# Window attention in the last two layers: copies on the DMA queue, squares after the rotation, masks before the wait for q and k, weights first on GpSimd

## The reference, cut to what is computed here

```
h = shift_token(x)                      # upper 64 features come from the token before
q, k, v = split(h @ wqkv)               # 8 heads of 64 numbers each
q, k = l2norm(q) * q_scale, l2norm(k) * k_scale
q, k = rotary_xpos(q, k)                # q * cos + rotate_half(q) * sin, with scales
# windows of 64 tokens; a query sees its own window and the one before
sim  = 8 * q . k, masked outside i - 64 <= j <= i
o    = softmax(sim) @ v
x    = x + o @ wo
h    = layernorm(shift_token(x)) @ w1 + b1
a, g = split(h)
x    = x + (a * gelu(g)) @ w2 + b2
```

## Time and profile before

| | us |
|---|---|
| median of 3 runs | 1512.03 |
| lowest and highest | 1510.12, 1512.65 |
| the profiled execution, its own time | 1508.53 |
| its span (first to last instruction) | 1506.5 |
| PE busy | 1333.5 (89%) |
| DVE busy | 1013.3 (67%) |
| ACT busy | 792.7 (53%) |
| POOL busy | 361.6 (24%) |

### The profile page before, as it was taken

How to read it: one execution, slowest core, us unless ns; L and a number is a source line. 1 busy time by engine, 2 the same in 40 slices (tenths; PEclk the granted TensorE clock), 3 DMA queues, 4 the chain that set the end, 5 groups by cost and what they waited for, 6 DMA issues and landing times.

```text
span 1506.5 us, 23829 instructions
## 1 busy us (share of the span) xinstructions
PE 1333.5 (89%) x9009; PEld 790.8 (52%) x9009; DVE 1013.3 (67%) x2202; ACT 792.7 (53%) x1681; POOL 361.6 (24%) x288
## 2 busy tenths in 40 slices
PE   6999999999999999999589999987279988799886
PEld 4767677776777673333223333333146654366652
DVE  5767767687766856765577667740967775877755
ACT  4544435444444442434136666675169984499851
POOL 0000000011000003335410000000267771477732
PEclk9999999999999999999569999999589999999998
DMA  5000000000000000002023111100200000000000
GB/s 141 1 1 1 1 1 1 1 1 1 1 1 1 0 1 1 1 0 81 29 77 82 46 37 37 36 3 7 57 1 2 2 2 1 1 2 2 2 1 28
DMA packets 23725, 26.03 MB, mean 17 GB/s; under 512 B 5602, under 2 KB 20140, under 8 KB 22316
## 3 DMA queue, kind: packets, MB, share of 16 engines
q1 hardware_dynamic: 23612, 24.51, 5.5%
HBM read 20.11 MB, written 4.39 MB: 16 GB/s over the span
## 4 chain that ended last, share of the span: by engine, by line
PE 64%; ACT 14%; DVE 13%; issue 4%; POOL 2%; DMA 2%; SPq 0%; POOLq 0%; DVEq 0%; ACTq 0%
PE ps L679 13%; PE ps L699 8%; PE ps L714 7%; ACT probsT L2283 6%; PE ps L1051 4%; PE ps L1010 4%; PE ps L1031 3%; DVE negmax L1437 2%; PE ps L888 2%; PE ps L882 2%; PE ps L1182 2%; PE ps L650 2%; ACT v_st L2253 2%; PE ps L1173 2%; PE ps L872 2%
## 5 line engine op out<-in xcount | busy, mean ns | idle before, releaser
L2208 ACT ACTIVATE probsT<-ps 128x512 f32<-128x512 f32 (+1 forms) x304 | 163.6, 576 | 103.7 <-PE ps L1035 91.6
L1437 DVE TENSOR_REDUCE negmax<-ps 128x1 f32<-128x1024 f32 x128 | 150.7, 1219 | 72.5 <-PE ps L699 72.4
L2030 ACT ACTIVATE probs<-ps,negmax 128x1024 f32<-128x1024 f32 x128 | 142.5, 1114 | 80.5 <-DVE negmax L1437 76.5
L2036 ACT COPY probsT<-ps 128x512 f32<-128x512 f32 x128 | 74.8, 584 | 168.2 <-PE ps L714 168.1
L714 PEld LDWEIGHTS ps<-ident,probs 128*128 128x128 f32 x1024 | 114.5, 141 | 66.2 <-issue 44.0
L714 PE MATMUL ps<-ident,probs 128*128 128x128 f32 x1024 | 138.4, 277 | 6.6 <-DVE probsT L1450 3.4
L2360 POOL TENSOR_SCALAR rstd<-mv 128x4 f32<-128x4 f32 (+1 forms) x23 | 5.3, 233 | 578.5 <-DVE mv L1372 578.4
L1010 PE MATMUL ps<-arena 76*128 76x512 bf16 (+3 forms) x384 | 113.6, 355 | 26.4 <-DVE cmax L1705 20.6
L699 PE MATMUL ps<-k_st,q_st 64*128 64x512 f32 x512 | 128.7, 622 | 5.9 <-ACT probs L2030 5.9
L1705 DVE CUSTOM_DVE_ANT_0 k_st<-ps,rel 128x256 f32<-128x256 f32 (+7 forms) x128 | 96.8, 756 | 44.1 <-PE ps L1010 43.2
L1705 DVE CUSTOM_DVE_ANT_0 q_st<-ps,rel 128x256 f32<-128x256 f32 (+7 forms) x128 | 96.7, 756 | 41.9 <-PE ps L1010 41.0
(11 more groups left out here) (245 smaller groups left out, 2565.1 us busy)
## 6 DMA issues: line engine op xcount, KB each, us to landing
arena<-c_parts SPq DMA_DIRECT2D x32, 192.0 KB
arena<-c_parts SPq DMA_DIRECT2D x16, 128.0 KB
arena<-in_L_ffn_w_dram SPq DMA_DIRECT2D x3, 512.0 KB
c_parts<-probsT SPq DMA_DIRECT2D x2, 768.0 KB, 3.5
arena<-in_c_far_dram SPq DMA_DIRECT2D x16, 96.0 KB
c_parts<-work SPq DMA_DIRECT2D x2, 768.0 KB, 11.3
work<-in_L_ffn_wqkv_dram SPq DMA_DIRECT2D x1, 1536.0 KB
x_sb<-in_L_attn_x_dram SPq DMA_DIRECT2D x2, 512.0 KB, 5.9
```

What stands on the lines that cost most here:

```text
L1437: dve.tensor_reduce(negmax[:, u:u + 1], s2, AX_X, ALU.max, negate=True).then_inc(s_a_negmax, 1)
L2030: act.activation(probs[:, u % NPB, :], s2, ACT.Exp, bias=negmax[:, u:u + 1], accum_out=rowsum[:, u:u + 1]).then_inc(s_a_exp, 1)
L2208: act.activation(c_p[:, kt % 2, j0:j0 + heads, q0 - kt * P:q0 - kt * P + n], ps[:, 4 + c % 2, 0:heads * n].rearrange("p (h n) -> p h n", n ...
```

## The change

- `d_vs` is no longer written by ACT. SP issues two DMAs for each tile: rows 0 to 63 from `d_va` of the tile, and rows 64 to 127 from `d_va` of the tile before. A new semaphore `s_d_vs` counts them; `shifted(n)` is its value when all copies of the tiles before tile n have landed. ACT waits for `shifted(n)` before it writes `d_va` of tile n, since the copies of tile n - 1 read the buffer that is written. PE waits for it ahead of the weights times v. `s_d_v` now comes with the one remaining copy.
- `square` moves on ACT from behind the exponentials to behind the value copy, for tile t + 2 instead of t + 3, and waits for the rotation (`s_d_m`) instead of the projection. `rotate` on DVE waits for the projection (`s_d_qkp`) instead of the squares. `norms` waits for the squares, and stands behind the addition to x.
- On PE the waits for turned q and k move from ahead of the two mask matmuls to behind them. The wait for `s_d_e` stays ahead.
- On POOL `unit_norm` loses its first addition, which becomes `add_queries`. A step is now: weights of tile t, power and scaling of tile t + 2, and then the addition of q for tile t + 3. `add_keys` and `add_queries` wait for `s_d_qkt`, the turn of the tile that used the buffer before.

```diff
--- before.py
+++ after.py
@@ -422,6 +422,7 @@
         s_d_kT = sem("s_d_kT")
         s_d_v = sem("s_d_v")
         s_d_addk = sem("s_d_addk")
+        s_d_vs = sem("s_d_vs")
         s_d_s = sem("s_d_s")
         s_d_nm = sem("s_d_nm")
         s_d_nm8 = sem("s_d_nm8")
@@ -453,6 +454,13 @@
         STACK = 16 * 9
 
         block = ctx.enter_context(nc.Block())
+
+        def exists(t, shift):
+            return 0 <= t + shift < TILES
+
+        def shifted(n):
+
+            return 16 * (2 * n - (n + TILES - 1) // TILES)
 
         @block.sync
         def _(sp):
@@ -550,6 +558,18 @@
                 for m, w in enumerate(("L1_ffn_q_scale", "L1_ffn_k_scale")):
                     sp.dma_start(qk_scale[:, l, m, :], a[w][l].partition_broadcast(P)).then_inc(s_ld_d, 16)
 
+            for l in range(DEPTH):
+                for t in range(TILES):
+                    n, par = TILES * l + t, t % 2
+                    sp.wait_ge(s_d_v, n + 1)
+                    if exists(t, -2):
+                        sp.wait_ge(s_d_o, n - 1)
+                    if n:
+                        sp.wait_ge(s_d_vs, shifted(n))
+                    sp.dma_start(d_vs[0:WIN, par, :], d_va[0:WIN, par, :]).then_inc(s_d_vs, 16)
+                    if exists(t, -1):
+                        sp.dma_start(d_vs[WIN:P, par, :], d_va[WIN:P, 1 - par, :]).then_inc(s_d_vs, 16)
+
             for b in range(BATCH):
                 for g in range(HALF):
                     sp.wait_ge(s_res, group_no(3, b, g))
@@ -560,8 +580,6 @@
 
         NU = 2 * QT
 
-        def exists(t, shift):
-            return 0 <= t + shift < TILES
 
         def ring(j):
 
@@ -1151,8 +1169,6 @@
                             pe.wait_ge(s_d_v, n)
                         pe.matmul(ps[:, 3, :], hT[:, WIN + t * P:WIN + (t + 1) * P], w4qkv[:, l, 2 * INNER:3 * INNER],
                                   start=True, stop=True).then_inc(s_d_vp, 1)
-                        pe.wait_ge(s_d_qT, n + 1)
-                        pe.wait_ge(s_d_kT, n + 1)
                     if exists(t, 0):
 
 
@@ -1162,6 +1178,8 @@
                             pe.matmul(ps[:, 6 + i, :].rearrange("p (h c) -> p h c", c=P), ident_b[:, :],
                                       mask_b[:, t:t + 1, :].to_broadcast([P, 4, P]),
                                       start=True, stop=False, skip_group_check=True)
+                        pe.wait_ge(s_d_qT, n + 1)
+                        pe.wait_ge(s_d_kT, n + 1)
                         for h in range(H2):
                             r, m = HD2 * (h % 2), h // 2
 
@@ -1199,6 +1217,7 @@
 
                         pe.wait_ge(s_d_pTa, n)
                         pe.wait_ge(s_d_pT, n)
+                        pe.wait_ge(s_d_vs, shifted(n))
                         pe.wait_ge(s_d_v, n)
                         if exists(t, -2):
                             pe.wait_ge(s_d_oT, n - 1)
@@ -1774,7 +1793,7 @@
 
                         return v.rearrange("p t n d -> p n t d").to_broadcast([P, 2, H2, v.shape[3]])
 
-                    dve.wait_ge(s_d_sq, n + 1)
+                    dve.wait_ge(s_d_qkp, n + 1)
                     if exists(t, -2):
                         dve.wait_ge(s_d_add, n - 1)
                     dve.tensor_tensor(mA, qk, heads(rot_c[:, t:t + 1, :, :]), ALU.mult)
@@ -1785,12 +1804,15 @@
 
             def add_keys(l, t):
                     n, par = TILES * l + t, t % 2
+                    if exists(t, -2):
+                        dve.wait_ge(s_d_qkt, n - 1)
                     dve.wait_ge(s_d_m, n + 1)
                     dve.tensor_tensor(d_kq[par][:, INNER:2 * INNER], d_mA[:, par, INNER:2 * INNER],
                                       d_mB[:, par, INNER:2 * INNER], ALU.add).then_inc(s_d_addk, 1)
 
             def norms(l, t):
                     n, par = TILES * l + t, t % 2
+                    dve.wait_ge(s_d_sq, n + 1)
                     dve.tensor_reduce(ss[:, par, :], d_sq[:, par, :].rearrange("p (h d) -> p h d", d=HD2),
                                       AX_X, ALU.add).then_inc(s_d_ss, 1)
                     dve.wait_ge(s_d_ss, n + 1)
@@ -1799,6 +1821,7 @@
 
             def step(l, t, piece=None):
                     n, par = TILES * l + t, t % 2
+
                     if exists(t, 2):
                         rotate(l, t + 2)
                     if exists(t, 0):
@@ -1816,12 +1839,13 @@
                            .then_inc(s_d_pT, 1)
                     if exists(t, 2):
                         add_keys(l, t + 2)
-                        norms(l, t + 2)
                     if exists(t, -2):
 
                         dve.wait_ge(s_d_w, n - 1)
                         z = xT[:, (t - 2) * P:(t - 1) * P]
                         dve.tensor_tensor(z, ps[:, 3, 0:P], z, ALU.add).then_inc(s_d_z, 1)
+                    if exists(t, 2):
+                        norms(l, t + 2)
                     if piece:
                         piece()
                     if exists(t, 0):
@@ -1936,9 +1960,9 @@
                     last_norm(0)
                 else:
                     add_keys(l + 1, 0)
-                    norms(l + 1, 0)
                 gated(l, 10)
                 if not last:
+                    norms(l + 1, 0)
                     next_shift(l, 1)
                 gated(l, 11)
                 add_down(l, 2)
@@ -2249,7 +2273,7 @@
                     n, par = TILES * l + t, t % 2
                     if exists(t, -2):
                         act.wait_ge(s_d_ss, n - 1)
-                    act.wait_ge(s_d_qkp, n + 1)
+                    act.wait_ge(s_d_m, n + 1)
                     act.activation(d_sq[:, par, :], ps[:, 0:2, :].rearrange("p n c -> p (n c)"), ACT.Square)\
                        .then_inc(s_d_sq, 1)
 
@@ -2267,12 +2291,14 @@
                     if piece:
                         piece()
                     if exists(t, 0):
-                        if exists(t, -1):
-                            act.wait_ge(s_d_v, n)
-                            act.copy(d_vs[WIN:P, par, :], d_va[WIN:P, 1 - par, :])
                         act.wait_ge(s_d_vp, n + 1)
-                        act.copy(d_va[:, par, :], ps[:, 3, :])
-                        act.copy(d_vs[0:WIN, par, :], ps[0:WIN, 3, :]).then_inc(s_d_v, 1)
+                        if n >= 2:
+                            act.wait_ge(s_d_vs, shifted(n))
+                        if exists(t, -2):
+                            act.wait_ge(s_d_o, n - 1)
+                        act.copy(d_va[:, par, :], ps[:, 3, :]).then_inc(s_d_v, 1)
+                    if exists(t, 2):
+                        square(l, t + 2)
                     if exists(t, -1):
                         act.wait_ge(s_d_pt, n)
                         act.copy(d_pT[:, 0:4, :].rearrange("p h c -> p (h c)"), ps[:, 4, :]).then_inc(s_d_pTa, 1)
@@ -2285,8 +2311,6 @@
                                                  scale=d_rn[:, par, hd:hd + 1],
                                                  accum_out=d_sum[:, par, h:h + 1])
                         ins.then_inc(s_d_e, 1)
-                    if exists(t, 3):
-                        square(l, t + 3)
 
 
             def ffn_yT(l, c):
@@ -2307,7 +2331,7 @@
 
             for l in range(DEPTH):
                 if l == 0:
-                    for t in range(3):
+                    for t in range(2):
                         square(l, t)
                 for t in range(15):
                     step(l, t)
@@ -2328,12 +2352,11 @@
                     if j == 6:
                         ffn_yT(l, 3)
                     if l + 1 < DEPTH:
-                        if j == 8:
+                        if j == 9:
                             square(l + 1, 0)
                 if l + 1 < DEPTH:
                     square(l + 1, 1)
                     act.activation(tpre[:, 1:2], eps_c[:, 0:1], ACT.Exp)
-                    square(l + 1, 2)
 
 
         @block.gpsimd
@@ -2477,33 +2500,47 @@
 
             pool.wait_ge(s_d_init, 1)
 
-            def unit_norm(l, t):
+            def add_queries(l, t):
 
                     n, par = TILES * l + t, t % 2
                     kq = d_kq[par]
                     pool.wait_ge(s_d_m, n + 1)
+                    if exists(t, -2):
+                        pool.wait_ge(s_d_qkt, n - 1)
                     pool.tensor_tensor(kq[:, 0:INNER], d_mA[:, par, 0:INNER], d_mB[:, par, 0:INNER], ALU.add)\
                         .then_inc(s_d_add, 1)
+
+            def unit_norm(l, t):
+
+                    n, par = TILES * l + t, t % 2
                     pool.wait_ge(s_d_cl, n + 1)
                     pool.tensor_tensor(d_rn[:, par, :], ss[:, par, :], half_c[:, :], ALU.pow).then_inc(s_d_rn, 1)
                     pool.wait_ge(s_d_addk, n + 1)
+                    pool.wait_ge(s_d_add, n + 1)
                     pool.wait_ge(s_d_rn, n + 1)
-                    v = kq[:, INNER:2 * INNER].rearrange("p (h d) -> p h d", d=HD2)
```

(27 more changed lines are left out.)

## The result

The changed kernel takes 1488.61 us (median of 4 runs, 1487.84 to 1488.89) where before takes 1512.12 (4 runs). The ratio is 0.9846, 95% interval 0.9829 to 0.9863: 23.5 us faster. 22.5 were forecast, 1489.5 us, in a range of 1484 to 1500.

The account below looks back on a forecast made before the run. A ring of waits through PE and ACT bounds the 9.04 us step, then PE's 8.41. 15.1 + 3.4 + 1.6 + 2.3 + 2.0 - 1.9 = 22.5 us off the median 1512.03 gives 1489.5, range 1484 to 1500.

Parts of the forecast that it names:

- twelve steps a layer, tile 1 to 13: Steady steps of both layers: each falls from 9.04 to 8.41 us, 15.1 in all; the second interval gives 0.3 more a layer.
- first interval, tile 0 to 1: Between the first two tiles, where PE has no output or weighted values to compute: 1.4 us less a layer.
- late steps, tile 13 to 15: Two steps a layer without projection of q and k: masks go under PE's wait for k, 4 x 0.4 = 1.6 us.
- from tile 15's maxima on, both layers: Tile 15 without half copies on ACT saves 2.3 us; between layers, rotations no longer behind the squares save 2.0.
- layer starts, meetings: Cost at layer starts: sums wait for later squares, 0.4 to 0.5 us each, and DVE and POOL meet; taken as 1.9.
- the ring: PE and ACT wait for each other: exponentials, squares, q/k copies, masks, scores, weights' turn and copy; 9.04 us falls to 7.6.
- The step, 8.41: Steady step after the change: PE is full and sets it at its own busy time, 8.41 us instead of 9.04.
- The bounds of the terms: Uncertainties: PE's step may be 8.3, 2.6 us less in all; TensorE's clock is worth some 2.5 us either way.
- Squares: On ACT, moved behind the value copy: 0.91 us leave the ring, at no cost while 0.6 us to spare lasts.
- Masks: On PE, ahead of the wait for k: 0.53 us leave the ring; that wait goes, with 0.1 us to spare.
- Copies: Half copies by DMA: ACT loses about 1.1 us a step; they land in 2.3 to 4 us, cost zero.
- Weights first: POOL's new order: power 1.2 us earlier; scaling meets DVE's addition of keys; cost zero in steady steps, 0 to 1 at starts.

## Why the prediction was right, point by point

By the maxima in the two profiles, in us over both layers:

| term | forecast | measured |
|---|---|---|
| twelve steps a layer, tile 1 to 13 | 15.1 + 0.6 | 19.0 |
| first interval, tile 0 to 1 | 2.8 | 2.6 |
| late steps, tile 13 to 15 | 1.6 | -4.2 |
| from tile 15's maxima on, both layers | 4.3 | 5.9 |
| layer starts, meetings | -1.9 | -0.6 |
| sum | 22.5 | 22.7 |

The measured column is of one profile of each kernel, and two of its rows don't compare like with like. The start of the second layer is in the row of tile 15. And the 2.6 of the first interval, where 1.4 a layer were forecast, are 2.5 in the first layer and 0.1 in the second; in the first layer the granted clock of that interval was 0.83 before and 0.97 after. That row is right by luck.

**The bound.** Right: the ring was the limit, its members were the squares and the masks, and PE's own list took over. The kernels with one part each show both limits.

**The step, 8.41.** Missed by 0.15 us; the twelve steps brought 19.0 instead of 15.1 + 0.6, 3.3 more. The term that was mis-sized is "PE is full and sets the step: 8.41". It took PE's busy time beside a wait for the length of its list without one, and there the v projection counts 1.02, against 0.86 when the masks follow at once. The bounds of the terms had 8.3.

**Squares.** Right in the sum (they cost nothing in their new place, the squares start at 1173.70 and end at 1174.73, 0.48 ahead of the copy), but "the ring loses 0.91" holds only together with the masks. There is a shorter ring, turn of q and k, two copies, masks, that the squares are not on.

**Masks.** Right: the wait is gone, with 0.14 us between the end of the copy of k and the scores. Counted as the forecast counts, both sides came shorter: PE reaches the scores 2.34 us behind the start of the turn (1172.93 - 1170.59; 2.48 forecast), and k is there after 2.20 + 0.10 = 2.30 (2.35 forecast). So 0.04 us were to spare and not 0.1.

**Copies.** Right that they land in time (2.5 us) and that their new waits cost nothing. "ACT does not bind then" is right because of this part: with the copies back the step is 8.49. As a term of the steady step they were given nothing, and they bring 0.23.

**Weights first.** The step that failed is "cost zero". The steady step pays nothing, as DVE had 1.14 us to give, but the meeting I named was the lesser one. The addition of keys, which was to take 1.0 to 1.3 us, took its 0.68 as before; it began first, and POOL's scaling took 1.40 instead of 1.04. The one I didn't see was the clamp. The Trainium skill's page "SBUF — State Buffer", section "Who interferes with whom", names `tensor_scalar` among the instructions that can contend with GpSimd, when their operands meet its conditions; the trace agrees, 0.81 us instead of 0.17. In the late steps, where VectorE has no wait to give, such meetings reach PE (below): two of its waits in the first layer are 1.77 and 1.04 us, with GpSimd's old order 1.42 and 0.25.

**Late steps.** The largest miss, and the step of the prediction that failed here: it counted only the 0.35 to 0.5 us of masks that leave PE's wait for k, and got -4.2 for 1.6, 5.8 us on the wrong side. The waits ahead of the masks did go. Three things came in their place. PE's timeline in the first layer, before and then after:

```profile
1228.22 0.66 PE L1219 MATMUL ps<-ident,arena 128*128 128x128 f32 x4 [1.09 <-DVE arena L1754]
...
1234.89 1.17 PE L1208 MATMUL ps<-probsT 128*64 128x64 f32 x32 [0.25 <-issue]
...
1239.11 0.66 PE L1227 MATMUL ps<-ident,xn 128*128 128x128 f32 x4 [3.04 <-DVE xn L1844]
1239.60 1.04 PE L1143 MATMUL ps<-ident,k_st 128*128 128x128 f32 x8
1240.47 1.02 PE L1152 MATMUL ps<-work,arena 128*128 128x512 f32 x2
```

```profile
1221.15 0.66 PE L1238 MATMUL ps<-ident,arena 128*128 128x128 f32 x4 [1.77 <-DVE arena L1773]
...
1228.11 1.17 PE L1227 MATMUL ps<-probsT 128*64 128x64 f32 x32 [1.04 <-issue]
...
1232.32 1.12 PE L1246 MATMUL ps<-ident,xn 128*128 128x128 f32 x4 [3.05 <-DVE xn L1868]
1233.23 1.91 PE L1161 MATMUL ps<-ident,k_st 128*128 128x128 f32 x8
1234.94 1.92 PE L1170 MATMUL ps<-work,arena 128*128 128x512 f32 x2
```

First, PE waits 1.77 us instead of 1.09 for DVE's copy of x into the shifted input (L1773). The clamp stands two copies ahead of it and takes 0.85 us there (from 1219.48) beside POOL's addition, 0.68 more than alone. Second, in both layers a scaling of the maxima (L1832) runs beside POOL's scaling of k; timelines of DVE and POOL in the first layer:

```profile
1226.44 0.96 DVE L1832 SCALAR_TENSOR_TENSOR d_nm<-d_nm,d_rn 128x8 f32<-128x8 f32 x1
...
1226.34 1.04 POOL L2522 TENSOR_TENSOR k_st<-k_st,d_rn 128x512 f32<-128x512 f32 x1 [0.17 <-POOL d_rn L2517]
```

It takes 0.96 us instead of 0.17, ahead of the exponentials and of DVE's copy of turned weights, and PE's wait ahead of the weights times v (at 1228.11) is 1.04 us instead of 0.25. Third, TensorE's granted clock falls in the first layer too, which only the second did before. Busy times by stretch, before and then after:

```profile
1233.00:1244.00 11.00, 7.36 (x115) 5.73 (x114) 7.45 (x30) 6.51 (x22) 7.28 (x7) 1.00 0.01 2
```

```profile
1226.00:1240.00 14.00, 9.91 (x115) 7.45 (x114) 8.16 (x30) 6.71 (x22) 5.63 (x7) 0.76 0.08 19
```

The turn takes 1.91 us where it took 1.04 at 2.4 GHz, the projection 1.92 instead of 1.02: 1.2 GHz. From the turn of `xn` to the maxima of tile 15 it is 6.83 us (1232.32 to 1239.15), where it was 4.54 (1239.11 to 1243.65). The wait ahead is 3.05 us, the same as before (3.04), when the clock stayed up. Of the 3.25 us by which tile 13 to 15 grew in the first layer, 0.68 and 0.79 are then the two waits and 2.3 the slower stretch, less 0.5 for the wait at the masks and the closer groups. The forecast had the clock as a bound of 2.5 us either way. In the second layer, where the clock is down in both kernels, the growth is 0.9.

Why the clock falls now is open. It falls somewhere between tile 13 and 15 of the first layer in all twelve other profiles, those of before with one part alone among them. So the profile of before may be the exception, and part of the loss no cost of the change; no run shows which. The kernels without L1832's meeting take 21.25 us (old order) and 21.8 (clamp moved) for tile 13 to 15 of the first layer, still above the 20.4 of before. In both the clock falls too, and PE's wait for L1773 is 1.42 and 1.86 us, so that the excess can't be given to one of the two.

So the number is right to 1 us partly by luck: the late steps came out 5.8 us worse than taken, the twelve steps 3.3 better, what follows tile 15 1.6 better and the start 1.3 better.

## What to carry to other kernels

In a loop over several engines, write down the rings and the list of each engine, and take the largest. A part's worth is its length only while its ring stays the largest; here 0.91 us of squares brought 0.27 alone and 0.16 on top of the others. When a small instruction is placed anew on VectorE, look at what GpSimd runs beside it: here two instructions of 0.17 us took 0.80 (median) and 0.96. Moving the clamp to GpSimd made the kernel 2.5 us faster, by the medians on one chip, but the next copy in VectorE's list was then the one that met GpSimd. A move of data off a busy engine onto a DMA queue is free as long as the wait that it brings has a whole step to be met, and that margin can be measured by making the copy two and three times.

## What the runs showed of the hardware

A copy of 64 rows of 2 KB within SBUF took 2.5 us (median) from its issue to its landing, and two of them behind one another took 2.87 from the first issue to where the next round could be issued. In the meetings of GpSimd and VectorE read here the instruction that began second became longer, by nearly as much as the first still had to run: POOL's scaling by 0.36 us, where VectorE's addition had 0.49 left, and VectorE's clamp by 0.64, where GpSimd's addition had 0.77 left. TensorE ran a whole step of 8.26 us without a gap at a granted clock of 1.00. The same wait of TensorE was followed by a granted clock of 1.00 in one kernel and of 0.76 in the other (3.04 and 3.05 us). The part of the program ahead of the two layers varied by 3.6 us between profiled executions (the memset starts at 1072.7 to 1076.3), while the two layers of the changed kernel took 411.1 and 411.2 in its two profiles.
